# Last stage of a fused kernel: gain rows by a one-hot product on normalised columns

## What is computed

```python
x = x + attn(cond(x))                 # stages before, unchanged
# last stage, x is now x1:
h = ln(x, pw_g[pathway_ids], pw_b[pathway_ids])
h = ln(h, cp_g[compartment_ids], cp_b[compartment_ids])
t = ln(x, tm_g[time_steps], tm_b[time_steps])          # 5 rows
m, n, r = (x + mlp_ln(state_i)[:, None, :] for i in 3 states)
s = ln(x, ms_g[scale_type], ms_b[scale_type])          # 3 rows
cat = concatenate([w[0]*h, w[1]*t, w[2]*m, w[3]*n, w[4]*r, w[5]*s])
u = ln(silu(cat @ int_W1 + int_b1) @ int_W2 + int_b2) * int_g + int_be
q = clip(round(u / rowscale), -127, 127); q_rhs likewise per column
x = x + (q @ q_rhs) * rowscale * rhs_scale
# ln(x, g, b) = (x - mean) * rsqrt(var + 1e-5) * g + b ; w = softmax(aw)
```

## Time and profile before

| | us |
|---|---|
| median of 3 runs (1743.07 to 1749.94) | 1745.22 |
| the profiled execution | 1745.17 |
| its span in the trace | 1743.3 |
| last stage, from the first step of block 0 to the end | 1209.6 to 1743.3 |

### The profile page before, as it was taken

The page is one execution under the profiler, slowest core; times in us unless marked ns, Lnnn a source line. Parts: engine busy times, 40 slices in busy tenths (PEclk is TensorE's granted clock), DMA queues, the critical chain, the costliest instruction groups (busy, mean ns, idle before and its releaser), DMA issues. The chain is left out here.

```text
span 1743.3 us, 23362 instructions
## 1 busy us (share of the span) xinstructions
PE 1731.6 (99%) x7935; PEld 1408.6 (81%) x7935; DVE 1192.5 (68%) x1756; ACT 875.4 (50%) x1299; POOL 789.0 (45%) x702
## 2 busy tenths in 40 slices
PE   9999999999999999999999999999999999999998
PEld 7888888888888888888888888778887787788786
DVE  7766666669989688785563335357886687577565
ACT  7655556565666665674562223243453443443433
POOL 1122221222686566665560000015577877878742
PEclk9999999999999999999999999999999999999999
DMA  6011100120243334222536568877645445544511
GB/s 208 1 49 49 48 21 27 49 73 25 97 142 121 124 103 163 97 97 89 187 136 224 192 199 283 325 253 244 222 138 180 140 161 174 157 158 151 162 47 61
DMA packets 121992, 234.36 MB, mean 134 GB/s; under 512 B 25619, under 2 KB 25875, under 8 KB 121893
## 3 DMA queue, kind: packets, MB, share of 16 engines
q1 hardware_dynamic: 91732, 157.63, 27.1%
q0 software_dynamic: 11776, 41.95, 7.2%
q10 hardware_dynamic: 18384, 33.56, 5.6%
HBM read 170.71 MB, written 58.72 MB: 132 GB/s over the span
## 5 line engine op out<-in xcount | busy, mean ns | idle before, releaser
L1081 PE MATMUL bank<-h_parts,mlp_w 128*128 128x512 f32 x2016 | 459.3, 389 | 0.6 <-ACT product_copy L1301 0.5
L1081 PEld LDWEIGHTS bank<-h_parts,mlp_w 128*128 128x128 f32 x2016 | 378.1, 188 | 80.4 <-ACT product_copy L1301 1.4
L358 PE MATMUL bank<-h_parts,gate_w 128*128 128x512 f32 x1536 | 351.1, 389 | 0.6 <-DVE h_parts L695 0.6
L358 PEld LDWEIGHTS bank<-h_parts,gate_w 128*128 128x128 f32 x1536 | 288.1, 188 | 61.9 <-issue 0.9
L2085 PE MATMUL bank<-operand_parts,int_w 128*128 128x512 f32 x1152 | 279.0, 395 | 0.1
L1146 PE MATMUL bank<-p_parts,mlp_out_w 128*128 128x512 f32 x1152 | 267.4, 391 | 0.0
L1146 PEld LDWEIGHTS bank<-p_parts,mlp_out_w 128*128 128x128 f32 x1152 | 214.7, 188 | 48.0 <-issue 2.5
L2085 PEld LDWEIGHTS bank<-operand_parts,int_w 128*128 128x128 f32 x1152 | 212.5, 188 | 45.5 <-issue 1.7
L620 POOL TENSOR_TENSOR decay_sq<-decay 128x512 f32<-128x512 f32 x32 | 39.2, 1226 | 278.8 <-DVE decay L708 278.8
L1422 POOL TENSOR_TENSOR product_out<-product_out,gelu 128x512 f32<-128x512 f32 x69 | 119.7, 1756 | 96.8 <-DVE product_out L1581 96.2
L1301 ACT ACTIVATE product_copy<-bank,vec_sb 128x512 f32<-128x512 f32 x144 | 99.1, 688 | 106.4 <-PE bank L1081 105.3
(11 more groups left out here) (311 smaller groups left out, 2755.8 us busy)
## 6 DMA issues: line engine op xcount, KB each, us to landing
p_tile<-p_d ACTq DMA_DIRECT2D x96, 256.0 KB, 4.9
p_d<-product_out SPq DMA_DIRECT2D x92, 256.0 KB, 2.0
raw_mlp_w<-mlp_gate_g SPq DMA_DIRECT2D x21, 512.0 KB, 3.6
raw_mlp_w<-mlp_fc_g SPq DMA_DIRECT2D x21, 512.0 KB, 4.1
xin<-xT SPq DMA_DIRECT2D x8, 1024.0 KB
hs_d<-u SPq DMA_DIRECT2D x8, 1024.0 KB, 5.0
hs_pair<-hs_d SPq DMA_DIRECT2D x8, 1024.0 KB, 7.6
x_columns<-xT SPq DMA_DIRECT2D x8, 1024.0 KB, 6.7
```

What stands on the lines that cost most here:

```text
L358: i = pe.matmul(bank[:], gw[:, w, s, k, m * P:(m + 1) * P], hr[:, q, t, k, :], start=k == 0 and n == 0, stop=k == KT - 1 and n == 2)
L1081: i = pe.matmul(bank[:], wb[g % 2][:, s, w, kk, :], hop[u % 2][o][:, t, kk, :], start=first and kk == 0 and n == 0, stop=kk == 1 and n == ...
```

## The change

The time and scale gain rows are no longer gathered row by row for each token. A table `gains` (high and low parts of the 5 time rows and the 3 scale rows, by groups of 128 channels, in the four partition groups) is multiplied by the one-hot matrix on TensorE (items `tt` and `ts`), which gives the gains with channels on the partitions; VectorE multiplies them with normalised x columns (`gain_product`) into `tn` or, for s, in place in `xn`. The normalised columns are made by GpSimd from the x columns that are loaded anyway (`xhat_columns`: a product with the row's rsqrt and an addition of its shift, both spread over the partitions). For the spreading the statistics of the next block are transposed by TensorE (`turn_stats`, in the place of an unused item), copied by ScalarE, stored to `stats_d` and loaded back to all partitions by SyncE. `gather_ts`, `scale_rows`, `t_product` and the transposes of t and s go. Items 8 to 11 are issued ahead of main 6 (in block 0 behind it) and 12 to 15 ahead of main 10; the bias moves from step 8 to step 10. The loads of x columns also wait for GpSimd's product on the old ones. The order of several other works changes, as the core of the diff shows:

```diff
@@ operands of the time (t) and scale (s) steps
-            if kind in ("th", "tt", "ts"):
-                pe.wait_ge(S[{"th": "h_prod", "tt": "t_prod", "ts": "s_prod"}[kind]], TT * (b + 1))
+            if kind == "th":
+                pe.wait_ge(S["h_prod"], TT * (b + 1))
...
+            elif kind in ("tt", "ts"):
+                if isinstance(b, int) and b == 0:
+                    pe.wait_ge(gain_done, 1)
+                pe.wait_ge(S["oh_done"], b + 1)
+                group, c = gain_of(kind, k)
+                i = pe.matmul(dst[:], gains[group, c, :], oh[group, :], start=True, stop=True, tile_position=(group.start, 0))
@@ order of the items on TensorE
+    ITEMS_AT = {2: (4, 5), 4: (6, 7), 6: (8, 9, 10, 11), 10: (12, 13, 14, 15)}
+    GAINS_AT = {6: (8, 9), 7: (10, 11), 10: (12, 13), 11: (14, 15)}
+    BIAS_AT = 10
+    FIRST_STAT_QT, FIRST_STAT_AT = 1, 9
+    STAT_QT, STAT_AT = 2, 11
@@ TensorE: statistics transposed, for the next block
+        def turn_stats(b, n, prev):
+            wait_bank(b - 1, n, prev, True)
+            pe.wait_ge(S["x_rs"], 2 * (b + 1))
+            pe.transpose(bank_of[n][0:2 * TT, 0:P], rs[:, XS].rearrange("p c t -> p (c t)"), ident[:]).then_inc(stat_ps, 1)
@@ ScalarE
+        def stats_out(b):
+            act.wait_ge(stat_ps, b + 1)
...
+            act.activation(stat_rows[0:2 * TT, :], bank("qt", ...)[0:2 * TT, 0:P], ACT.Copy).then_inc(stat_rows_done, 1)
...
+                if m == 2 and centre_next:
+                    h_centre(b + 1, [0, 1])
@@ SyncE
             residual(0)
             residual(1)
-            turn(0)
+            for t in range(TT):
+                turn(t)
+            if nxt:
+                store_stats(b + 1)
+                load_stats(b + 1)
             if nxt2:
                 sp.wait_ge(S["xh_done"], TT * (b + 2))
                 load(b + 2)
-            for t in range(1, TT):
-                turn(t)
@@ GpSimd
-        def scale_rows(b):
-            pool.wait_ge(S["xh_done"], TT * (b + 1))
-            pool.wait_ge(ts_rows, 16 * TT * (b + 1))
-            for t in range(TT):
-                pool.tensor_tensor(gts[t][:, 1], gts[t][:, 1], xh[:, t, :], ALU.mult).then_inc(S["s_prod"], 1)
+        def xhat_columns(b, k):
...
+            pool.wait_ge(stats_loaded, 32 * (b + 1))
+            pool.tensor_tensor(by_tile(xn[:, k]), by_tile(x_columns(b, k)), spread_of(0), ALU.mult).then_inc(xn_mul, 1)
+            pool.wait_ge(xn_mul, KT * b + k + 1)
+            pool.tensor_tensor(by_tile(xn[:, k]), by_tile(xn[:, k]), spread_of(1), ALU.add).then_inc(xn_add, 1)
...
             if prev:
-                scale_rows(b)
+                xhat_columns(b, 2)
+                xhat_columns(b, 3)
...
             if nxt:
-                for t in range(TT):
-                    gather_ts(b + 1, t, t == 0)
+                xhat_columns(b + 1, 0)
+                xhat_columns(b + 1, 1)
...
+            rsqrt(HS, "h_ve", "h_rs", b)
             for t in range(TT):
                 gather_cp(b, t)
-            if prev:
-                rsqrt(HS, "h_ve", "h_rs", b)
@@ VectorE
+        def gain_product(b, s):
+            o, k = steps[s]
+            dve.wait_ge(S[FRONT[o] + "_ps"], KT * b + k + 1)
+            dve.wait_ge(xn_add, KT * b + k + 1)
+            dve.tensor_tensor(source(b, s), xn[:, k], bank(FRONT[o], k)[:], ALU.mult).then_inc(S[o + "_prod"], 1)
...
         def front_low(b, s):
...
-            dve.tensor_tensor(op[:, s % 4, 1, :], x_columns(b, k) if o == "x" else bank(FRONT[o], k)[:],
-                              op[:, s % 4, 0, :].bitcast(F32), ALU.subtract).then_inc(S["op_low"], 1)
+            dve.tensor_tensor(op[:, s % 4, 1, :], source(b, s), op[:, s % 4, 0, :].bitcast(F32), ALU.subtract).then_inc(S["op_low"], 1)
@@ VectorE, steps_of
-                if T_AT <= s < T_AT + TT:
-                    t_product(b, s - T_AT)
+                for later in GAINS_AT.get(s, ()):
+                    gain_product(b, later)
+                if s == XF + 1:
+                    front_low(b, s + AHEAD)
                 if nxt and X_AT <= s < X_AT + TT:
                     x_moments(b + 1, [s - X_AT])
+                if s == XF:
+                    front_low(b, s + AHEAD)
@@ VectorE, first_steps (block 0)
             x_moments(1, [3])
-            for t in range(TT):
-                t_product(0, t)
+            gain_table()
+            one_hot(0)
             front_low(0, 6)
             front_low(0, 7)
-            for t in range(TT):
-                s_product_first(t)
             split_low(*SLOT[1], [0])
-            one_hot(0)
             split_low(*SLOT[2], [0])
             split_low(*SLOT[1], [1])
+            gain_product(0, 8)
+            gain_product(0, 9)
             front_low(0, 8)
             front_low(0, 9)
+            gain_product(0, 10)
+            gain_product(0, 11)
             rhs_maximum()
+            front_low(0, 10)
+            front_low(0, 11)
+            rhs_peak()
             split_low(*SLOT[2], [1])
             split_low(*SLOT[1], [2])
             table_rows_now(1)
-            front_low(0, 10)
-            front_low(0, 11)
             split_low(*SLOT[2], [2])
-            rhs_peak()
...
             split_second(0)
+            gain_product(0, 12)
+            gain_product(0, 13)
             front_low(0, 12)
             front_low(0, 13)
             h_moments(1, [2])
+            gain_product(0, 14)
+            gain_product(0, 15)
             front_low(0, 14)
```

More of the change, by code:

```diff
@@ L1834, in add_items @@
         o, k = steps[s]
-        items.append((FRONT[o], k, ("op_low", NS, s, 0)))
+        items.append((FRONT[o], k, {"h": ("op_low", NS, s, 0), "t": ("t_prod", KT, k, 0), "s": ("s_prod", KT, k, 0)}[o]))
     order = []
     for s in range(NS):
-        if s % 2 == 0 and XF <= s + AHEAD < NS:
-            for ahead in (AHEAD, AHEAD + 1):
-                add_items(s + ahead)
-                order.append(("item", len(items) - 1))
+        for later in ITEMS_AT.get(s, ()):
+            add_items(later)
+            order.append(("item", len(items) - 1))
         order.append(("main", s))
@@ L1920, in body @@
             else:
[L1921 removed]
+                tail(b, nxt, nxt2)
         def early_small():
@@ L2385, in body @@
                     split_high(2)
+                if not prev and s == 3:
+                    act.wait_ge(gain_loaded, 16)
+                    act.activation(gain_hi[:], gain_raw[:], ACT.Copy).then_inc(gain_high, 1)
                 if not prev and s == ABS_AT:
```

223 lines of the change are left out of this document (139 added, 84 removed).

## The result

| | us |
|---|---|
| median after (4 runs, 1772.68 to 1777.54) | 1774.16 |
| median before (4 runs, 1743.07 to 1749.94) | 1747.01 |
| ratio | 1.0164, 95% interval 1.0149 to 1.0179 |
| the profiled execution after | 1773.7, span 1771.9 |

The changed kernel is 1.6% slower; 1735 was forecast, with a range to 1748. The page of after, part 1, is the counterpart of the earlier trace rows: TensorE has less work, VectorE 77 us more, GpSimd 30 us more.

What follows compares the result with a forecast made beforehand. TensorE, 99% busy, was taken as the bound. Savings of 16.9 us in seven blocks, less 1.4 for stalls and 5 in block 0, took 1745.2 to 1734.7, so 1735 us; range 1728 to 1748.

Steps and rivals of the forecast that it cites:

- TensorE's saving: Transposes of t and s go, one-hot multiplications come: net 2.43 us less a block (2.1 to 2.6).
- the first one-hot group: Four short one-hot multiplications alone between mains 5 and 6 on TensorE: 0.66 us.
- Second group and bias together: Four one-hot multiplications directly ahead of the bias at step 10: 0.36 us added, sharing the bias's two drains.
- The transpose of the statistics: One added TensorE transpose in each of blocks 0 to 6: 0.11 us.
- VectorE's added work: Gain products for t products: +1.9 us; low parts of t and s from SBUF: up to 4.3 more, within idle.
- VectorE at the block's end: Stall allowance covering tight steps 6 and 7 and the block's end: 0.2 us a block, 0 to 1.
- Rival three: GpSimd's SBUF operations at the block's end starve VectorE at the port: +3.7 us a block, 1759; chance 0.12.
- GpSimd at nothing: GpSimd's round of 60 to 62.8 us against a beat of 61.6, costed at nothing.
- The reordered h square root: On GpSimd, moved ahead of the cp gathers: a wait of 2 us or so for VectorE's last h statistics.
- The statistics' way and SyncE: Transpose, copy, store and broadcast load hidden with 9 us or more to spare; SyncE's reordered transfers hidden as well.
- Block 0: First block: main 11 waits about 5 us for gain product 12's bank; block ends 5 us later (3.5 to 7).
- rival four: One-hot groups don't run side by side on TensorE: 1.8 us in place of 1.0, 1740.5; chance 0.05.

Runs made afterwards that it cites:

- experiment eleven: Changed kernel without GpSimd's x scaling (t and s terms not computed) and with the silu written to banks: 1727.05 us, kernel before 1746.97.
- nine: Changed kernel with silu in banks, two h products behind the sum of u, cp gathers before the h square root, tail additions before x scaling: 1749.46 us.
- seven: Changed kernel with silu in banks and two of the four h products moved behind the sum of u: 1750.20 us.
- twelve: As nine, with low parts 8 and 9 made earlier in VectorE's list: 1747.75 us, ratio to the kernel before 1.0004.
- experiment two: Changed kernel with the cp gathers put back ahead of the h square root: 1757.21 us.
- four: Changed kernel with the silu written to two banks, so hidden low parts have one SBUF input: 1747.98 us.
- six: Changed kernel with only VectorE's list in the first block reordered, gain products 12 and 13 directly behind the rhs peak: 1775.96 us.
- experiment three: Changed kernel with two x scalings moved between the h rows and the h square root, all four tail additions together: 1763.69 us.
- ten: As nine, with the third and fourth x scaling held until VectorE's last h product: 1756.03 us.

## Why the prediction was wrong

**TensorE's saving: right.** 2.43 was forecast with 2.1 to 2.6; 2.64 is measured where nothing disturbs it (experiment eleven). By the rows above, the first one-hot group costs 1437.23 - 1431.15 - 5.55 = 0.53 (0.66 forecast). Second group and bias together cost 1449.01 - 1437.23 - 2 x 5.45 = 0.88, or 0.78 with 5.55 for the first 24 (1.02 forecast), less than 0.53 + 0.66 apart, as if two groups in a row shared what it costs to enter and leave them. The transpose of the statistics is 0.11, as forecast.

**VectorE's added work: size right.** A gain product takes 683 ns (683 forecast), the low parts of t and s 832 and 1372 (1222 forecast for both). Experiment eleven shows that they cost no time in blocks 1 to 7 when GpSimd does not scale beside them; in nine, a low part of s that met GpSimd took 1.76, and TensorE waited for it.

**VectorE at the block's end: the step that failed.** "I set 0.2 us a block for this and the block's end" stands against 6.9 us in truth: 68.36 less the 61.44 of an undisturbed block. The step weighed the low parts in the middle of the block, where the margin seemed thin, and gave the end nothing of its own. In truth the middle held until the end was mended (seven, nine), and the end broke. Rival three describes what happened, place, operations and port; it stood at 0.12. The prediction's reason against its price was that a low part of x costs on average only 0.54 more from SBUF. But that mean is a mix of operations that met GpSimd and others that did not; this is the spread of the same twelve in the kernel before (min/median/max):

```profile
L2711 DVE TENSOR_TENSOR operand_parts<-x_columns,operand_parts x12: 676/792/3184, 1470.0 to 1655.7; 128x512 fp32r<-128x512 f32 x12
```

That row, and the 693 against 3453 of the hidden ones in the earlier trace rows, were the warning: the maximum was the price of a meeting, and the change made the meetings regular. Rival three's own size (a beat some 1.3 above the old one, 4.3 measured) was too small for three reasons. Eight operations met GpSimd's row, not six, and lost 16.8 - 5.5 = 11.3 us instead of 7.7. The hidden low parts stalled TensorE themselves, 2.78, besides the sum of u, 2.69. And the clock fell behind the waits, which cost some 1.5 us in each block (7.33 against 5.71 for 24 multiplications), up to 2.9 (8.62, at 1554.75).

**GpSimd at nothing: not the bound of the changed kernel, but wrong as an agent.** After the change GpSimd waited 2.65 for the h statistics (2 forecast) and was busy for 52 to 54 us of 68. It was never what TensorE waited for. Whether it would have let TensorE run at 61.6 is another matter: with the meetings at the end mended, the kernel that computes all its terms settled at 64.1 (twelve), and the part of GpSimd's chain in that is open. At the block's end the forecast counted its new operations only as time on GpSimd (10.4 to 12.5; 12.6 measured, eight at 1.58) and as a price on GpSimd, 0.3 us for each meeting. The price fell on VectorE. The reordered h square root, priced at "a wait of 2 us or so", was worth 17 us of the total (experiment two), since the wait moved GpSimd's row onto the hidden low parts.

**The statistics' way and SyncE: right.** No wait for the spread statistics shows on GpSimd, and none for x1 on VectorE.

**Block 0: mechanism right, size short.** The wait is where it was forecast, ahead of main 11, for the bank of gain product 12: 5.35 against 5. The last four steps started 5.4 us later than before, near the forecast 5. With main 11 at 5.08 in place of 3.0, at the lower clock, that took up the whole of the forecast. Then the block ended 7.6 later (8.8 longer, from an earlier start), since three waits for hidden low parts add 0.38, 0.64 and 0.76 at its end. With the silu in a bank alone block 0 takes 70.9 (four), and without GpSimd's scaling as well 69.1 (eleven), still 3.9 more than before. Moving the product earlier moves the wait but not the block's length (six), and which of VectorE's works would have to leave block 0 stays open.

**What the sum would have been.** With the measured terms: 6 x (6.9 - 2.64) = 25.6, -2.6 for block 7 and +8.8 for block 0 make 31.8. The span grew by 28.6. The difference is the earlier start of the stage (1.2) and the old blocks 1 and 2, which together took 2.3 more than twice 64.03. (A slip without weight: by its own terms rival four comes to 1734.7 + 7 x 0.8 = 1740.3, not 1740.5.)

## What to carry to other kernels

When work moves to GpSimd, list what VectorE does at the same moment, and mark the operations with two inputs in SBUF: each may last as long as GpSimd's operation beside it (1.7 us here), or as two of them (3.2). A gather issued by GpSimd is not the same neighbour as an elementwise operation, even if it takes about as long: before the change three of the four hidden low parts of a block ran while GpSimd issued gathers, and took 0.69. Look at the longest of a group, not only at its mean. The cheapest cure was not to move the work but to give the victim one input in a bank (26 us). A rare long maximum of a cheap operation in the old trace is the price of a meeting that the change may make regular.

## What the hardware showed unexpectedly

- VectorE operations with two SBUF inputs, beside an unbroken row on GpSimd, take 1.7 us each on average (1771 for h products, 688 without the row in experiment three), and 3.2 each for the two that meet a pair of tail additions (6.48 for two). GpSimd's own operations grow only from 1.26 to between 1.6 and 1.74. The loss is not shared equally.
- The clock level of 1.2 GHz came after waits of 2.69 and 2.59 at a block's end, and in experiment nine after 1.83 in mid-block (12 multiplications in 4.59, not 3.0), but not after 2.04 in experiment four, where 24 multiplications took their 5.71. After the same wait of 2.78 in the second product it came at the end of three blocks and not at the end of three others. The length of the one wait does not decide it alone.
- A wait taken away at one spot came back elsewhere in five of the experiments (three, six, seven, nine, ten): as a gather, as hidden low parts, as an output store, as low parts in mid-block, as an operand.
